# An attention and expert kernel: stacks, gathers and shift rows moved in fewer transfers over interleaved rows

## The reference

```
x = x + _layernorm(_L0_attn_ref(_layernorm(x), ...))     # 8 batches, 1024 tokens, 16 heads of 16
    q = heads(x @ q_w.T + q_b) / 4;  k, v likewise
    attn = softmax(einsum("bhqd,bhkd->bhqk", q, k))
    out = einsum("bhqk,bhkd->bhqd", attn, v) ... @ out_w.T + out_b
x = x + _layernorm(_L0_ffn_ref(_layernorm(x), ...))      # 16 experts, top 8, shared expert
```

## Time and profile before

| | |
|---|---|
| median of three runs | 2877.35 us |
| the profiled execution | 2881.35 us |
| its span in the trace | 2879.6 us |
| attention, from the first P·V matmul to the last | 104.6 to about 1673 us |
| one batch of attention | 193.6 to 201.0 us |

### The profile page before, as it was taken

The page is one execution under the profiler, slowest core; times in us unless marked ns, Lnnn a source line. Parts: engine busy times, 40 slices in busy tenths (PEclk is TensorE's granted clock), DMA queues, the critical chain, the costliest instruction groups (busy, mean ns, idle before and its releaser), DMA issues.

```text
span 2879.6 us, 49724 instructions
## 1 busy us (share of the span) xinstructions
PE 2694.3 (94%) x17634; PEld 1769.8 (61%) x17634; DVE 2208.8 (77%) x4585; ACT 1628.8 (57%) x3159; POOL 1039.2 (36%) x1057
## 2 busy tenths in 40 slices
PE   4999999999989999999998899999999999999997
PEld 2434444444444444444443378888888888888886
DVE  4798898899989988988988767666666666666664
ACT  1477777777777777777777853333333333333332
POOL 4042572553544534735635655111111111111112
PEclk8799999999999999999999999999999999999999
DMA  5203414333233134133243233232222222232221
GB/s 93 49 27 56 64 42 71 57 72 64 61 62 64 42 64 64 41 65 63 47 76 85 76 89 89 82 81 82 78 80 74 76 82 81 79 81 78 82 71 55
DMA packets 136649, 197.46 MB, mean 69 GB/s; under 512 B 22337, under 2 KB 84817, under 8 KB 134353
## 3 DMA queue, kind: packets, MB, share of 16 engines
q1 hardware_dynamic: 136400, 194.29, 30.7%
HBM read 108.74 MB, written 17.30 MB: 44 GB/s over the span
## 4 chain that ended last, share of the span: by engine, by line
PE 58%; DVE 16%; SPq 16%; POOL 4%; issue 3%; DMA 1%; ACT 1%; POOLq 0%; ACTq 0%; DVEq 0%
PE y_bank L748 13%; PE g_bank L734 13%; DVE score_max L1119 13%; PE u_bank L734 13%; SPq L350 9%; PE o_bank L574 7%; PE sm_bank L564 6%; PE st_bank L551 3%; SPq L363 2%; SPq L374 2%; SPq L375 2%; SPq L354 1%; DVE qk_parts L1141 1%; POOL recip_tmp L1506 1%; POOL recip L1511 1%
## 5 line engine op out<-in xcount | busy, mean ns | idle before, releaser
L1119 DVE TENSOR_REDUCE score_max<-sm_bank 128x1 f32<-128x512 f32 x2048 | 1280.2, 682 | 173.5 <-PE sm_bank L564 169.9
L1011 ACT ACTIVATE probs<-st_bank 128x512 f32<-128x512 f32 x2023 | 1078.7, 603 | 338.1 <-PE st_bank L551 330.1
L564 PE MATMUL sm_bank<-qk_stack 64*128 64x512 f32 x2048 | 828.7, 467 | 86.3 <-DVE score_max L1119 71.4
L551 PE MATMUL st_bank<-qk_stack 64*128 64x512 f32 x2023 | 757.4, 433 | 30.1 <-DMA qk_stack<-shift_row 28.3
L564 PEld LDWEIGHTS sm_bank<-qk_stack 64*128 64x128 f32 x2048 | 371.3, 191 | 461.6 <-DVE score_max L1119 420.9
L574 PE MATMUL o_bank<-probs,v_quad 128*32 128x512 f32 x4096 | 559.5, 619 | 17.8 <-DMA qk_stack<-qk_stack 16.4
L551 PEld LDWEIGHTS st_bank<-qk_stack 64*128 64x128 f32 x2023 | 358.6, 189 | 262.1 <-ACT probs L1011 188.6
L1266 DVE TENSOR_TENSOR h<-gate_act,u_bank 128x512 f32<-128x512 f32 x256 | 176.2, 688 | 311.0 <-ACT gate_act L966 310.9
L966 ACT ACTIVATE gate_act<-g_bank 128x512 f32<-128x512 f32 x272 | 162.8, 598 | 415.6 <-PE u_bank L734 415.5
L977 ACT ACTIVATE h_hi<-h 128x512 fp32r<-128x512 f32 x272 | 172.1, 633 | 327.5 <-DVE h L1269 289.8
L1549 POOL TENSOR_SCALAR f_x_in<-f_x_in,f_mv,f_rstd 128x256 f32<-128x256 f32 x64 | 90.5, 1423 | 620.4 <-DVE f_rstd L1180 620.4
(11 more groups left out here) (216 smaller groups left out, 4377.9 us busy)
## 6 DMA issues: line engine op xcount, KB each, us to landing
cb<-comb_dram SPq DMA_DIRECT2D x256, 256.0 KB, 3.7
qk_stack<-qk_parts SPq DMA_DIRECT2D x360, 128.0 KB
x_in<-in_x SPq DMA_DIRECT2D x8, 1024.0 KB, 5.7
o_part<-o_sb SPq DMA_DIRECT2D x256, 32.0 KB, 1.9
sum_part<-o_sb SPq DMA_DIRECT2D x256, 32.0 KB, 1.9
x_res<-in_x SPq DMA_DIRECT2D x16, 512.0 KB, 3.9
x<-x_res SPq DMA_DIRECT2D x16, 512.0 KB, 3.3
f_x_in<-x SPq DMA_DIRECT2D x16, 512.0 KB, 4.0
```

Source lines behind the costliest of these rows:

```text
L551: mm(bank_of(tile)[:, :], k_stack[q][p][rows, kc * CH:(kc + 1) * CH], q_stack[q][p][rows, f * HALF:(f + 1) * HALF], start=True, stop=True) ...
L564: mm(sm_bank[n % RING][:, :], q_stack[q][p][rows, tok:tok + CH], k_stack[q][p][rows, half * HALF:(half + 1) * HALF], start=True, stop=True ...
L1011: nc.scalar.activation(probs[kc % 2][:, HEAD_AT[j], :], bank_of(4 * U + j)[:, :], ACT.Exp).then_inc(exp_done, 1)
L1119: v.reduce_max(score_max[f][:, HC * (2 * p + e) + c, half:half + 1], sm_bank[n % RING][:, :], AX_X).then_inc(smax_read, 1)
```

## The change

The rows of a stack are interleaved: a head's partition 4d + t holds part t of dimension d, so t = 0, 1, 2 are the three pairs of parts, and t = 3 holds the shift in the first row and zeros in the others. Two neighbouring heads of a pair then fill partitions t, t + 4, ... up to 127 from 32 neighbouring partitions of `qk_parts` in one transfer. A stack is six transfers of 32 partitions and one of two zero rows, which now comes first. It counts on two semaphores, one for each pair; PE waits for the first pair where it waited for the stack, and for the second pair four units later. A shift row takes two transfers of two partitions. `v_quad` has V and ones in alternating columns, so that `o_sb` has them in alternating rows, and a gather is two transfers of 64 partitions. Stack 1 of the next batch is issued ahead of the store of x1 instead of behind it.

```
-                for j in range(4):
-                    h, p, base = 4 * q + j, j // 2, 64 * (j % 2)
-                    src = slice(DH * (h % 8), DH * (h % 8) + DH)
-                    for rows, pair in ((0, slice(0, 4, 2)), (16, slice(1, 3)), (48, slice(0, 4, 3))):
-                        sp.dma_start(qk_stack[q][base + rows:base + rows + DH, p, :, :].bitcast(F32),
-                                     projected(B, m)[src, pair, :].bitcast(F32)).then_inc(stack_loaded[q], 16)
-                for base in (0, 64):
-                    sp.dma_start(qk_stack[q][base + 32:base + 33, :, 0, :].bitcast(F32),
-                                 qk_stack[q][base + 33:base + 34, :, 0, :].bitcast(F32)).then_inc(stack_loaded[q], 16)
+                sp.dma_start(qk_stack[q][SHIFT_ROW:SHIFT_ROW + 65:64, :, 0, :].bitcast(F32),
+                             qk_stack[q][ZERO_ROW:ZERO_ROW + 65:64, :, 0, :].bitcast(F32)).then_inc(stack_loaded[q][0], 16)
+                for p in range(2):
+                    at = DH * ((4 * q + 2 * p) % 8)
+                    for t, pair in enumerate((slice(0, 4, 2), slice(1, 3), slice(0, 4, 3))):
+                        sp.dma_start(qk_stack[q][t:128:4, p, :, :].bitcast(F32),
+                                     projected(B, m)[at:at + 2 * DH, pair, :].bitcast(F32)
+                                     ).then_inc(stack_loaded[q][p], 16)
...
-                for j in range(4):
-                    row = 64 * (j % 2) + 32
-                    sp.dma_start(q_stack[q][j // 2][row:row + 1, f * HALF:(f + 1) * HALF].bitcast(F32),
-                                 shift_row[f][HC * j:HC * (j + 1), :].bitcast(F32)).then_inc(shift_loaded, 16)
+                for p in range(2):
+                    sp.dma_start(q_stack[q][p][SHIFT_ROW:SHIFT_ROW + 65:64, f * HALF:(f + 1) * HALF].bitcast(F32),
+                                 shift_row[f][2 * HC * p:2 * HC * (p + 1), :].bitcast(F32)).then_inc(shift_loaded, 16)
...
-                for j in range(4):
-                    to = 64 * (q % 2) + DH * j
-                    sp.dma_start(o_part[f][to:to + DH, :], o_sb[32 * j:32 * j + DH, :]).then_inc(gathered, 16)
-                    sp.dma_start(sum_part[f][to:to + DH, :], o_sb[32 * j + DH:32 * j + 2 * DH, :]).then_inc(gathered, 16)
+                to = slice(64 * (q % 2), 64 * (q % 2) + 64)
+                sp.dma_start(o_part[f][to, :], o_sb[0:128:2, :]).then_inc(gathered, 16)
+                sp.dma_start(sum_part[f][to, :], o_sb[1:128:2, :]).then_inc(gathered, 16)
...
                 if not last:
                     load_stack(b + 1, 0, False)
+                    load_stack(b + 1, 1, False)
                 if not first:
                     store_x1(b - 1, 1)
-                if not last:
-                    load_stack(b + 1, 1, False)
...
+                    if s % 2 == 0 and kc % HC == 0 and maxima:
+                        B2, p = b if s < 6 else b + 1, kc // HC
+                        pe.wait_ge(stack_loaded[(s // 2 + 1) % QUADS][p], STACK_INC[p] * (B2 + 1))
...
-                g.tensor_copy(v_quad[q][:, :, :].rearrange("p c (h w) -> p c h w", h=4)[:, :, :, 0:DH],
-                              v_stage[:, :, 4 * q:4 * q + 4, :]).then_inc(v_copied, 1)
+                g.tensor_copy(v_quad[q][:, :, :].rearrange("p c (n t) -> p c n t", t=2)[:, :, :, 0],
+                              v_stage[:, :, 4 * q:4 * q + 4, :].rearrange("p c h d -> p c (h d)")).then_inc(v_copied, 1)
```

More of the change, by code:

```diff
@@ L18 @@
 VW = 2 * DH
+SHIFT_ROW, ZERO_ROW = 3, 7
 HEAD_AT = (1, 3, 0, 2)
@@ L218, in both_stages @@
         x1_stored = sem("x1_stored")
-        stack_loaded = [sem(f"stack_loaded{q}") for q in range(QUADS)]
+        stack_loaded = [[sem(f"stack_loaded{q}_{p}") for p in range(2)] for q in range(QUADS)]
         v_copied = sem("v_copied")
@@ L251, in nth @@
             return B * PER_BATCH[kind] + (i + 1)
-        GATHER_INC = 16 * 2 * 4
+        GATHER_INC = 16 * 2
         def split_no(B, f, k):
             return 4 * B + 2 * k + f
-        STACK_INC = 16 * (4 * 3 + 2)
+        STACK_INC = (16 * 4, 16 * 3)
         def over(place, used, name, shape, dt=F32):
@@ L542, in st @@
                 if kc == 0 and i == 0:
-                    pe.wait_ge(shift_loaded, 64 * (S + 1))
+                    pe.wait_ge(shift_loaded, 32 * (S + 1))
                 if tile >= LATE + 6:
@@ L765, in _ @@
             before.clear()
-            pe.wait_ge(stack_loaded[0], STACK_INC)
             for S in range(2):
                 for n in range(4 * CHUNKS):
+                    if n == 0 or n == 4 * HC:
+                        pe.wait_ge(stack_loaded[0][n // (4 * HC)], STACK_INC[n // (4 * HC)])
                     smax(S, S, n // 4, n % 4, False)
@@ L782, in batch @@
                     maxima = s + 2 < STEPS or not last
-                    if kc == 0 and s % 2 == 0:
-                        if maxima:
-                            B2 = b if s < 6 else b + 1
-                            pe.wait_ge(stack_loaded[(s // 2 + 1) % QUADS], STACK_INC * (B2 + 1))
+                    if s % 2 == 0 and kc % HC == 0 and maxima:
+                        B2, p = b if s < 6 else b + 1, kc // HC
+                        pe.wait_ge(stack_loaded[(s // 2 + 1) % QUADS][p], STACK_INC[p] * (B2 + 1))
+                    if s % 2 == 0 and kc == 0:
                         pe.wait_ge(v_copied, QUADS * b + s // 2 + 1)
@@ L875, in job @@
                         for q in ((2, 3) if m == 0 else (0, 1)):
-                            act.wait_ge(stack_loaded[q], STACK_INC * (B + m))
+                            for p in range(2):
+                                act.wait_ge(stack_loaded[q][p], STACK_INC[p] * (B + m))
                     nc.scalar.activation(half_of(B, i, 0), job_bank[:, :],
@@ L887, in job @@
                     if S > 1:
-                        act.wait_ge(shift_loaded, 64 * (S - 1))
+                        act.wait_ge(shift_loaded, 32 * (S - 1))
                     nc.scalar.activation(shift_row[f][:, :], job_bank[0:4 * HC, 0:CH], ACT.Copy,
@@ L926, in weight_hi @@
                     for q in (2, 3):
-                        act.wait_ge(stack_loaded[q], STACK_INC * BATCHES)
+                        for p in range(2):
+                            act.wait_ge(stack_loaded[q][p], STACK_INC[p] * BATCHES)
                 act.wait_ge(w_loaded[e], 48)
@@ L1006, in batch @@
                         if j == 0 and U == 0:
-                            act.wait_ge(stack_loaded[2], STACK_INC)
-                            act.wait_ge(stack_loaded[3], STACK_INC)
+                            for q in (2, 3):
+                                for p in range(2):
+                                    act.wait_ge(stack_loaded[q][p], STACK_INC[p])
                         if j == 0 and U >= 2:
```

## The result

The changed kernel took 2801.48 us, median of four runs (2798.07 to 2803.5), against 2876.82 us (2875.21 to 2879.11, four runs) for the kernel before: a ratio of 0.9736, 95% interval 0.9719 to 0.9753. The forecast was 2796.0 with a range of 2787 to 2815. The profiled execution took 2801.8 us, 79.6 us less than the profiled one of before.

What follows compares the result with a forecast made beforehand. The prediction took queue SP and the DMA engines behind it as the bound. Gains of 41.4 (B), 22.8 (A), 8.5 (C) and 8.5 (the start) sum to 81.2 us; off the median 2877.35 that forecast 2796, range 2787 to 2815.

Steps and rivals of the forecast that it cites:

- What bounds the kernel: Attention stage: queue SP plus the DMA engines behind it, not the data; PE waited 55.9 us on stacks and shift rows.
- The data rate: Data of two stacks: 15 to 20 us taken, between 26 us at 120 GB/s and 8.7 us at 363.
- B: Units 14 to 16, batches 1 to 7: shift row for step 2 no longer late behind two stacks, worth 41.4 us.
- A: Units 47 to 49, batches 0 to 6: no more wait for stack 0 of the next batch, worth 22.8 us.
- C: Units 54 and 55, batches 1 to 6: shift row for step 7 no longer behind stack 1; 9.2 us, counted 8.5.
- the start: Program start: PE's first maximum between 44.1 and 46.6 us instead of 53.55, a gain taken as 8.5 us.
- The base: Whole kernel: saving of 81.2 us taken off the median 2877.35 gives 2796.2; off the profiled 2881.35, 2800.2.
- Costs at nothing: GpSimd's copy of V, extra waits on PE and ScalarE, and the moved store of x1: no time lost.
- Rival 1: Part of the gain given back, shift rows still late at C or B: 2800 to 2820 us, middle 2808; chance 0.15.
- Rival 2: An issue's cost grows with its rows, so SP is held as long as before: 2849 us; chance 0.06.
- Rival 3: Slower: interleaved transfers at B run under 103 GB/s; about 3135 us at 60 GB/s; chance 0.04.
- Rival 4: More than forecast: units outside the three places speed up too, another 5 to 10 us: 2786 to 2791; chance 0.05.

Runs made afterwards that it cites:

- the repeat: The changed kernel run once more with nothing altered, on one chip beside the kernel before: 2797.56 us, ratio 0.9722.

## Why the prediction was right, and where it was off

**What bounds the kernel: right.** The queue SP and the data behind it set the shift rows and stacks late, and with that gone PE has no DMA wait in the batches. Holding the row back to unit 15 brought the stall back on its own.

**The data rate: right, at the fast end.** Forecast 15 to 20 us for two stacks; SP was held for 15.6, and the data took 16.8 us at the 187 GB/s of the trace, with 120 before. The rule of the Trainium skill ("SBUF — State Buffer", section on the DMA port swizzle), by which 32 neighbouring partitions reach twice as many ports as 16, gave the estimates of 218 GB/s and 14.5 us, 2.3 us less than the data took. The form with 16 neighbouring partitions in succession moved 134 GB/s, above the estimate of 109 but nearer to it than to 218. Here the trace agrees with the rule in direction and roughly in size.

**B: the term that was mis-sized.** I took 8.22 us of batch 0 as what units 14 to 16 take without a stall. They take 8.73 in batches 1 to 6 and 9.23 in batch 7. The rows had it: batch 0 has 14 VectorE instructions in the stretch, batch 1 has 20 and batch 7 has 25, since from batch 1 on the layer norm of the batch before runs there. VectorE is busy 8.43 of the 8.73 us. Six times 0.51 and once 1.01 are 4.1 us that were never there to gain: the term of 41.4 us measured 37.3.

**A: 1.5 us too little.** The 8.87 us of units 50 to 52 was a neighbouring place, not the same work; units 47 to 49 take 8.66. Seven times 0.21. The reason that the prediction gave, the first pair of heads early, was not needed: waiting for both pairs gave the same 8.66. The room of 6 us that it worked out was enough for the whole stack.

**C and the start: 0.7 too little, 0.3 too much.** The bounds of 44.1 and 46.6 us held the 45.36. There the split semaphore did its part, 3.6 of the 8.2 us, and the new transfers the rest.

**The base: the rest of the miss.** The corrected sum of 79.0 from the profiled 2881.35 gives 2802.4, and the profiled execution of after took 2801.8. From the median of 2877.35 it gives 2798.4, and the median was 2801.48. The profiled execution of before lay 4 us above its median, and the saving read from it was taken off the median whole. That the sum came so near rests in part on luck: 4.1 us too much at B stood against 1.5 and 0.7 too little at A and C. Whether taking the saving off the median was wrong can't be settled: the difference of medians was 75.3 us in the first comparison and 79.7 in the repeat, either side of 79.0 by no more than the scatter, so about 2 us of the miss of 5.5 are the terms and the remaining 3 are within what two comparisons of the same kernels differ by.

**Costs at nothing: right, with one qualification.** No PE wait names the copy of V. A copy has a median of 648 ns where it had 610, far from the doubling that I allowed for, and GpSimd's busy time rose by 3.3 us in all (1039.2 to 1042.5). The meeting of the seed with GpSimd in units 41 and 42 is not a cost of the change: in batch 1 of the kernel before the same operation took 1.22 us.

**Rivals.** Rival 1 (part given back) fell at B and C: even the gathers alone or the slower transfers left no wait. Rival 2 (an issue's cost grows with its rows) fell: a gather with 64 partitions was issued in 0.55 us (324.25 in the kernel with the old stacks). Rival 3 (slower below 103 GB/s) fell with 187 GB/s; the slowest form tried moved 134. Rival 4 (more than forecast) did not come by the change itself, only with the seed moved.

## What to carry to other kernels

When a queue is late by a few microseconds, the first few microseconds taken off it are worth all of the stall and the next ones nothing; so price each half of an edit alone, since here either half was enough. For the time without a stall take the same place in the same kind of batch, and compare the instruction counts in the two rows before you subtract. Behind each wait of 2 us or more on TensorE look at the granted clock: where it fell, a wait of 2.2 us cost 3.3 us or more, and where it did not, only itself.

## What the runs showed of the hardware that I had not expected

- A VectorE operation on 128 x 4 elements took 1.24 us instead of 0.17, and one on 128 x 16 took 1.53 us, each until a GpSimd operation that had started earlier was over, to within 0.03 us. In the Trainium skill, "SBUF — State Buffer", section "Who interferes with whom", VectorE and GpSimd share a pair of ports that the first one holds for a whole instruction, if the VectorE operation is of a kind that can use it or reads two operands from SBUF. Both pairs of rows agree in that the VectorE operation that started second ended with the GpSimd operation.
- A wait of PE's weight loads of up to 0.8 us for a shift row cost nothing in eight places. A wait of PE of 2.2 us cost 3.3 us with the clock at 0.50 for 3.4 us behind it, 4.6 us where the mean clock of the stretch was 0.74, and 2.3 us where the clock stayed at 1.00.
- Twelve transfers of the same shapes held SP for 10.97 us or 8.18 us for a stack, by their order alone; the DMA engines moved 134 or 179 GB/s.
